# A mixture of experts that scatters its weighted rows into the output itself

## The chip, the core and the metric

The kernel runs on one core of one Trainium2 chip. The core has five engines with queues of their own: TensorE (PE, with its weight loads as PEld), VectorE (DVE), ScalarE (ACT), GpSimd (POOL) and SyncE (SP), which here only issues transfers. They meet through semaphores alone. The metric is the time of one execution on the device in microseconds (us); lower is better.

## The reference

The program is a two-layer block over x of 16 x 128 rows of 256 numbers. Layer 0 is a cross attention and a quantised feed-forward part, layer 1 a cross attention in fp8 and a mixture of experts. Only the end of layer 1 is touched:

```python
x = x + jnp.tanh(g_xattn[1]) * _L1_xattn_ref(_layernorm(x, axis=-1), ctx_2048, ...)
x = x + jnp.tanh(g_ffn[1]) * _L1_ffn_ref(_layernorm(x, axis=-1), Wr, Win, Wout)

def _L1_ffn_ref(x, Wr, Win, Wout):
    logits = xf @ Wr.T
    scores, expert = jax.lax.top_k(logits, 2)
    weights = jax.nn.softmax(scores, axis=-1)
    gate = gate.at[jnp.arange(T)[:, None], expert].add(weights)
    for e in range(8):
        h = jax.nn.silu(xf @ Win[e].T)
        y = y + gate[:, e:e + 1] * (h @ Wout[e].T)
    return y.reshape(orig_shape)
```

So each of the 2048 rows goes to two of eight experts, and the result of a row is the attention's x plus two weighted rows.

## The kernel before, in words

x stays in SBUF for the whole program (`x_rows`, 128 partitions x 16 x 256 fp32). While the second attention ends, the rows are normalised, the two experts of each are chosen, and GpSimd scatters each row twice (once for each expert) as a packet of 259 numbers into `slots` in HBM, where every expert has a shelf. A packet carries the row's number, the first expert's code and the exponential of the gap of the scores. Slots that no row took hold a row number out of all bounds, so that a later scatter skips them. SP loads the experts' weights (8.4 MB) in 16 transfers into the place of the attention's weights.

`layer1_experts` then goes through 24 tiles: 15 wide ones of two blocks of 128 slots and 9 narrow ones of one. `SIZES` is that list and `RING` = 3 the number of buffers for loaded tiles, row numbers (`to_row`) and weighted rows (`slots_y`). A tile belongs to one expert, so no row stands in it twice. For each tile n:

- SP loads the packets (L2285). From the fourth tile on it waits until tile n - 3 is turned and its weights of the sum are worked out.
- TensorE transposes (`turn`, L2300), multiplies by the first matrix (`hidden`, L2322) and by the second (`down`, L2341). The order on TensorE is hidden(n+1), turn(n+2), down(n).
- VectorE copies the turned rows (`lift`), splits the hidden values in two halves (`parts`) and works out the target row and the share of each slot (`aim`, L2372 to L2386).
- ScalarE applies silu and writes the weighted rows to y (L2429).
- GpSimd scatters y (L2439), one indirect transfer for each block of 128 rows, into `picked` in HBM. `picked` has two halves of 2048 rows: a row's first expert writes into the first half, its second expert into the second. Hence no two scatters ever touch the same place, and none waits for another.

When all scatters have landed, SP and ACT read the two halves back in seven runs each (L2454), VectorE adds them to `x_rows` (L2475), and SP stores each run (L2461). The order on each engine is that in which the code is written. `v_x` is the semaphore that counts the finished pieces of `x_rows` in the second attention, J = 4 for each of 16 batch rows.

Of the kernel before, what the change touches and what calls it, by code (L numbers as in the profile page):

```python
# [14 lines left out]
F32 = mybir.dt.float32  # L15
# [4 lines left out]
U32 = mybir.dt.uint32  # L20
I32 = mybir.dt.int32

P = 128
B = 16
D = 256
# [187 lines left out]
def common_tiles(nc):  # L213

    t = {}
    t["x"] = nc.alloc_sbuf_tensor("x_rows", [P, B, D], F32)
    t["gates"] = nc.alloc_sbuf_tensor("gates", [P, 4], F32)
    t["ident"] = nc.alloc_sbuf_tensor("ident", [P, P], F32)
    t["ident_b"] = nc.alloc_sbuf_tensor("ident_b", [P, P], BF16)
    t["half"] = nc.alloc_sbuf_tensor("minus_half", [P, 16], F32)  # L220
    t["one_eps"] = nc.alloc_sbuf_tensor("one_eps", [P, 1], F32)
    t["eps_eps"] = nc.alloc_sbuf_tensor("eps_eps", [P, 1], F32)
    t["eps"] = nc.alloc_sbuf_tensor("eps", [P, 16], F32)
    t["token"] = nc.alloc_sbuf_tensor("token", [P, B], F32)
    t["blank"] = nc.alloc_sbuf_tensor("blank_slot", [P, SLOT], F32)
    t["slots"] = nc.dram_tensor("slots", [SLOTS, SLOT], F32, kind="Internal").ap()
    t["halves"] = nc.dram_tensor("halves", [2, P, 2, HALVES, HALF], F16, kind="Internal").ap()
    t["picked"] = nc.dram_tensor("picked", [2 * B * P, D], F32, kind="Internal").ap()
    number = nc.alloc_sbuf_tensor("token_number", [P, B], I32)
    t["wb"] = nc.alloc_sbuf_tensor("w_proj_in", [P, 2, UNITS, UNIT], F16)  # L230
    t["count"] = number
    t["most"] = nc.alloc_sbuf_tensor("most", [P, 2, B], F32)
    t["before"] = nc.alloc_sbuf_tensor("picks_before", [P, NE], BF16)
    t["shelf"] = nc.alloc_sbuf_tensor("shelf", [P, NE], F32)
    t["all_b"] = nc.alloc_sbuf_tensor("ones_b", [P, P], BF16)
    t["ident_h"] = nc.alloc_sbuf_tensor("ident_h", [P, P], F16)
    t["owner"] = nc.alloc_sbuf_tensor("tile_owner", [P, WORDS * WORD], F32)
    t["word"] = nc.alloc_sbuf_tensor("owner_word", [1, WORDS], I32)
    t["shelf_row"] = nc.alloc_sbuf_tensor("shelf_row", [1, WORDS * WORD], I32)
    return t  # L240
# [981 lines left out]
J = 4  # L1222
# [91 lines left out]
def layer1_attention(nc, a, t, ctx, bank, places, final, small):  # L1314
# [15 lines left out]
    x, gates, ident = t["x"], t["gates"], t["ident"]  # L1330
# [7 lines left out]
    rows, rowsT = over("bo0", "rows_n", [P, D]), over("q_part", "rowsT_n", [P, KD, P])  # L1338
# [7 lines left out]
    s = Pieces(nc)  # L1346
# [15 lines left out]
    pe_A, a_st, g_r = sigs("pe_A", "tensor", 4), sigs("a_st", "scalar", 3), [sig(f"g_r_{k}of3", "gpsimd", 2) for k in range(3)]  # L1362
    v_n, pe_hT, a_hT = sigs("v_n", "vector", 3), sigs("pe_headsT", "tensor", 3), sigs("a_headsT", "scalar", 3)
# [486 lines left out]
    def aside(owner):  # L1850
        return [("WP", n) for n in range(WP_EIGHTHS)] if (("WP", owner)) in s.pieces else []

    flags = {"pe_A": pe_A, "a_v": a_v, "a_hT": a_hT, "pe_out": pe_out, "r_c": r_c, "v_PT": v_PT, "v_go": v_go, "d_xs": d_xs}
    layer = Layer(s, lambda owner: part(owner, 1, 2), after,
                  lambda owner, b: rounds(ORDER1[owner], b, False), lambda owner: (2, B - AHEAD))
    return layer, starting, aside, rest_halves, flags, A, S, packet
# [381 lines left out]
TS = 2  # L2238
# [2 lines left out]
WORDS = -(-TILES // WORD)  # L2241


def layer1_experts(nc, block, a, t, out, ctx):
    def sb(name, shape, dt=F32):
        return ctx.enter_context(nc.sbuf_tensor(name, shape, dt))

    def sem(name):
        return nc.alloc_semaphore(name)

    x, gates, ident, token = t["x"], t["gates"], t["ident"], t["token"]
    slots, picked = t["slots"], t["picked"]
    win = t["win"].rearrange("p (h e k n) -> p h e k n", h=2, e=NE, k=KD)
    wout = t["wout"].rearrange("p (h e k n) -> p h e k n", h=2, e=NE, k=KF)
    ident_h = t["ident_h"]
# [7 lines left out]
    xT = sb("slotsT", [P, 2, 2 * KD * TS * P], F16)  # L2263
    h32, hh = sb("h32", [P, 2, KF * TS * P]), sb("hidden", [P, 2, 2, KF * TS * P], F16)
    y = sb("slots_y", [P, RING, TS, D])
    other, to = sb("other", [P, RING, TS]), sb("to_row", [P, RING, TS], U32)
    got, put = [sem(f"t_got{n}") for n in range(RING)], [sem(f"t_put{n}") for n in range(RING)]
    gate, part, both = sb("gate_part", [P, 1]), sb("part_of", [P, RING, TS]), sb("both_parts", [P, 2, TS])
    s_gate, s_part, c_part = sem("t_gate"), sem("t_part"), Chain(nc, "c_part", 3)
    s_turn, s_xT, s_to = sem("t_turn"), sem("t_xT"), sem("t_to")  # L2270
    s_H, s_h, s_hh, s_Y, s_y = sem("t_H"), sem("t_h"), sem("t_hh"), sem("t_Y"), sem("t_y")

    def puts(n):
        return 16 * sum(SIZES[n % RING:n:RING])

    @block.sync
    def _(e):
        e.wait_ge(t["tabled"], 1)
        e.wait_ge(t["sent"], 16 * 2 * B)
        for n, size in enumerate(SIZES):  # L2280
            if n >= RING:
                e.wait_ge(s_turn, n - RING + 1)
                e.wait_ge(s_part, n - RING + 1)
            row = e.value_load(shelf_row[0:1, n:n + 1], min_val=0, max_val=SLOTS - size * P)  # L2284
            e.dma_start(taken[:, n % RING, 0:size, :],  # L2285
                        slots[bass.ds(row, size * P), :].rearrange("(s p) w -> p s w", p=P)).then_inc(got[n % RING], 16)
# [70 lines left out]
    def _(e):  # L2357
# [7 lines left out]
        def aim(n):  # L2365
            e.wait_ge(s_gate, 1)
            e.wait_ge(s_part, n)
            size = SIZES[n]
            note = taken[:, n % RING, 0:size, :]
            if n >= RING:  # L2370
                e.wait_ge(put[n % RING], puts(n))
            e.tensor_scalar(other[:, n % RING, 0:size], note[:, :, D + 1:D + 2].rearrange("p s o -> p (s o)"),  # L2372
                            owner[:, n:n + 1], float(B * P), ALU.not_equal, ALU.mult).then_inc(s_to, 1)
            e.wait_ge(s_to, 2 * n + 1)
            e.tensor_tensor(to[:, n % RING, 0:size], note[:, :, D:D + 1].rearrange("p s o -> p (s o)"),
                            other[:, n % RING, 0:size], ALU.add).then_inc(s_to, 1)

            second = note[:, :, D + 2:D + 3].rearrange("p s o -> p (s o)")
            if n >= RING:
                e.wait_ge(s_y, n - RING + 1)  # L2380
            c_part.start(e, n)
            c_part.link(e.tensor_scalar(both[:, 0, 0:size], second, 1.0, None, ALU.add))
            c_part.link(e.reciprocal(both[:, 0, 0:size], both[:, 0, 0:size]))
            c_part.link(e.scalar_tensor_tensor(both[:, 1, 0:size], note[:, :, D + 1:D + 2].rearrange("p s o -> p (s o)"),
                                               owner[:, n:n + 1], second, ALU.is_equal, ALU.max))
            e.scalar_tensor_tensor(part[:, n % RING, 0:size], both[:, 1, 0:size], gate[:, 0:1], both[:, 0, 0:size],  # L2386
                                   ALU.mult, ALU.mult).then_inc(s_part, 1)
            c_part.end()
# [44 lines left out]
    @block.gpsimd  # L2433
    def _(e):
        for n, size in enumerate(SIZES):
            e.wait_ge(s_y, n + 1)
            e.wait_ge(s_to, 2 * n + 2)
            for h in range(size):
                e.indirect_dma_start(  # L2439
                    out=picked[:, :], out_offset=bass.IndirectOffsetOnAxis(ap=to[:, n % RING, h:h + 1], axis=0),  # L2440
                    in_=y[:, n % RING, h, :], in_offset=None, bounds_check=2 * B * P - 1,
                    oob_is_err=False).then_inc(put[n % RING], 16)


    RUNS = ((0, 1), (1, 3), (3, 6), (6, 10), (10, 13), (13, 15), (15, 16))
    back = t["wout"].bitcast(F32).rearrange("p (w b d) -> p w b d", w=2, b=B)
    s_back, s_sum, s_store = [sem(f"z_back{n}") for n in range(len(RUNS))], sem("z_sum"), sem("z_store")

    def read_back(e, which):
        for n in range(RING):  # L2450
            e.wait_ge(put[n], 16 * sum(SIZES[n::RING]))
        rows = picked.rearrange("(w b p) d -> w p b d", w=2, p=P)
        for n, (b0, b1) in enumerate(RUNS):
            e.dma_start(back[:, which, b0:b1, :], rows[which, :, b0:b1, :]).then_inc(s_back[n], 16)  # L2454

    @block.sync
    def _(e):
        read_back(e, 0)
        for n, (b0, b1) in enumerate(RUNS):
            e.wait_ge(s_sum, 2 * (n + 1))  # L2460
            e.dma_start(out[b0:b1].rearrange("b p d -> p b d"), x[:, b0:b1, :]).then_inc(s_store, 16)  # L2461
        e.wait_ge(s_store, 16 * len(RUNS))

    @block.scalar
    def _(e):
        read_back(e, 1)

    @block.vector
    def _(e):
        for n, (b0, b1) in enumerate(RUNS):  # L2470
            e.wait_ge(s_back[n], 32)
            for which in range(2):
                if which:
                    e.wait_ge(s_sum, 2 * n + 1)
                e.tensor_tensor(x[:, b0:b1, :], x[:, b0:b1, :], back[:, which, b0:b1, :], ALU.add).then_inc(s_sum, 1)  # L2475


def program(nc, a, out, phases):
# [23 lines left out]
        layers(block, first, second, between, closing, left, spent, cleared)  # L2502

    with ExitStack() as ctx:
        layer1_experts(nc, block, a, t, out, ctx)
    whole.close()
    kept.close()

# [67 lines left out]
```

## Time and profile before

| | us |
|---|---|
| median of 3 runs | 1259.28 (1255.86 to 1262.04) |
| profiled execution, its own time | 1258.14 |
| its span (first to last instruction) | 1256.2 |
| PE busy in the span | 1124.0 (89%) |
| DVE busy | 1039.6 (83%) |
| ACT busy | 918.5 (73%) |
| POOL busy | 748.0 (60%) |

Times of single events come from the profiled execution, counted from the first instruction. The median is 1.14 us above that execution's time, which in turn is 1.94 us above its span. A busy share is an average over the whole span: what a change at the end is worth has to be read from what ends last there.

### The profile page before, as it was taken

To read this page: it belongs to the slowest core of one execution; us is meant where nothing else is said; L and a number is where in the kernel's file an instruction comes from. 1 tells how busy PE (TensorE), PEld (TensorE's weight loads), DVE (VectorE), ACT (ScalarE), POOL (GpSimd) and SP (SyncE) were. 2 spreads that over 40 slices of the span, in tenths; PEclk is the share of its full clock that TensorE was granted. 3 is DMA by queue.
4 is the path that set the end of the run, shared out by engine and by line. 5 is a ranking of instruction groups with operands and counts; after the bars stand their busy time and mean duration, and the time that the engine had idled before them with its cause. 6 is when DMAs were issued, how large, how long until landed. Compare 5 with 4: busy or idle time off the path is not lost. (4 is left out here: it accounts for less than half of the span.)

```text
span 1256.2 us, 30380 instructions
## 1 busy us (share of the span) xinstructions
PE 1124.0 (89%) x8831; PEld 909.8 (72%) x8831; DVE 1039.6 (83%) x2469; ACT 918.5 (73%) x3601; POOL 748.0 (60%) x1132
## 2 busy tenths in 40 slices
PE   2689999978799999999999999998999999659992
PEld 2356666645688888888888888887887888559981
DVE  6689999987898888898898899888689888756664
ACT  3557777759899989989988998997888778223330
POOL 5368888867755665665566566565546787313331
PEclk8689999989999999999999999999999999879996
DMA  6555556531230330330230221122311000723326
GB/s 167 93 89 89 89 88 87 83 54 53 73 89 2 90 90 0 88 88 1 87 88 24 65 88 47 41 88 71 89 52 47 31 35 31 277 77 86 96 69 205
DMA packets 134167, 97.56 MB, mean 78 GB/s; under 512 B 54845, under 2 KB 127679, under 8 KB 134080
## 3 DMA queue, kind: packets, MB, share of 16 engines
q1 hardware_dynamic: 124528, 84.70, 27.7%
q0 software_dynamic: 3408, 8.45, 1.9%
q10 hardware_dynamic: 6144, 3.35, 0.9%
q8 instruction: 43, 0.70, 0.2%
q14 instruction: 44, 0.36, 0.1%
HBM read 55.02 MB, written 42.09 MB: 77 GB/s over the span
## 5 line engine op out<-in xcount | busy, mean ns | idle before, releaser
L1546 POOL TENSOR_TENSOR head_rstd<-head_rstd,minus_half 128x4 f32<-128x4 f32 x192 | 225.9, 1176 | 15.0
L1534 ACT ACTIVATE squares<-ps 128x128 bf16<-128x128 f32 x768 | 202.4, 285 | 42.2 <-PE ps L1497 34.8
L1497 PE MATMUL ps<-w_proj_in,xq 128*128 128x512 f16 (+1 forms) x1024 | 209.3, 327 | 5.9 <-ACT headsT L1570 5.3
L1626 POOL TENSOR_TENSOR prob<-prob,rinv 128x512 f32<-128x512 f32 x128 | 140.6, 1098 | 108.7 <-DVE rinv L1621 108.5
L1570 ACT ACTIVATE headsT<-ps,l_hln 128x256 f32<-128x256 f32 (+1 forms) x256 | 168.1, 690 | 30.3 <-PE ps L1561 30.3
L1613 ACT ACTIVATE prob<-ps,nmax 128x128 f32<-128x128 f32 x512 | 182.6, 391 | 9.7 <-DVE nmax L1604 8.3
L1534 ACT ACTIVATION_READ_ACCUMULATOR squares<-ps 128x1 f32 x768 | 165.2, 216 | 0.0
L1554 DVE TENSOR_TENSOR heads_n<-ps,head_rstd 128x512 f32<-128x512 f32 x192 | 131.3, 684 | 25.9 <-POOL head_rstd L1546 25.6
L1497 PEld LDWEIGHTS ps<-w_proj_in,xq 128*128 (+1 forms) x1024 | 99.9, 98 | 53.1 <-issue 8.5
L1597 PE MATMUL ps<-headsT 128*128 128x128 f32 x1024 | 137.0, 277 | 1.1 <-DVE probT L1642 0.4
L1544 POOL TENSOR_TENSOR head_rstd<-head_squares,l_head_eps 128x4 f32<-128x4 f32 x192 | 46.1, 240 | 151.9 <-ACT squares L1534 151.1
L1597 PEld LDWEIGHTS ps<-headsT 128*128 128x128 f32 x1024 | 128.9, 193 | 8.1 <-issue 5.5
L1653 PE MATMUL ps<-probT,v 128*128 128x256 f32 x512 | 132.4, 381 | 0.4 <-DVE x_rows L1133 0.4
L1702 PE MATMUL ps<-w_proj_out,catq 128*128 128x256 f16 x1024 | 123.7, 275 | 3.8 <-DVE catq L1690 3.8
L1561 PE MATMUL ps<-ident,heads_n 128*128 128x128 f32 x768 | 117.1, 275 | 5.9 <-DVE heads_n L1554 5.8
L1613 ACT ACTIVATION_READ_ACCUMULATOR prob<-ps,nmax 128x1 f32 x512 | 117.5, 230 | 0.0
L1604 DVE TENSOR_REDUCE nmax<-ps 128x4 f32<-128x512 f32 x128 | 88.1, 688 | 30.0 <-PE ps L1597 28.2
L1702 PEld LDWEIGHTS ps<-w_proj_out,catq 128*128 128x128 bf16 x1024 | 100.9, 99 | 15.8 <-DVE catq L1690 4.2
L1561 PEld LDWEIGHTS ps<-ident,heads_n 128*128 128x128 f32 x768 | 91.3, 142 | 23.7 <-DVE heads_n L1554 15.9
L1504 PE MATMUL ps<-w_proj_in,ctx_parts 128*128 128x256 f16 x768 | 104.8, 273 | 0.0
L852 DVE TENSOR_REDUCE nmax<-ps 128x4 f32<-128x512 f32 x128 | 83.3, 680 | 18.8 <-PE ps L844 18.5
L1653 PEld LDWEIGHTS ps<-probT,v 128*128 128x128 f32 x512 | 87.6, 191 | 7.2 <-issue 0.6
(320 smaller groups left out, 2588.1 us busy)
## 6 DMA issues: line engine op xcount, KB each, us to landing
slots<-blank_slot SPq DMA_DIRECT2D x12, 1554.0 KB, 8.5
halves<-half_made SPq DMA_DIRECT2D x32, 256.0 KB, 2.5
w_proj_in<-halves SPq DMA_DIRECT2D x16, 512.0 KB, 9.8
w_out_raw<-in_wprojT SPq DMA_DIRECT2D x8, 512.0 KB, 3.9
half_raw<-in_winT SPq DMA_DIRECT2D x16, 256.0 KB, 2.9
half_raw<-in_woutT SPq DMA_DIRECT2D x16, 256.0 KB, 3.1
taken<-slots SPq DMA_DIRECT2D x15, 259.0 KB, 3.4
q_rows<-q_parts SPq DMA_DIRECT2D x48, 64.0 KB
```

Of the source, the lines that this page charges most:

```text
L1497: last = e.matmul(out, xq[:, k, which, slot_at], weights(k, hl, c0, n), start=(k == 0 and hl == 0), stop=(k == KD - 1 and hl == 1))
L1504: last = e.matmul(out, cx[:, k, part, slot_at], weights(k, hl, c0, n), start=(k == 0 and part == hl == 0), stop=(k == KD - 1 and part == 1))
L1534: last = e.activation(squares[:, 4 * n + h, :], A[n][:, h * HD1:(h + 1) * HD1], ACT.Square, scale=HD1**-0.5, accum_out=hss[:, 4 * n + h:4 ...
L1546: e.tensor_tensor(hr[:, four], hr[:, four], t["half"][:, four], ALU.pow).then_inc(g_r[n].sem, 1)
L1554: e.tensor_tensor(hn[:, n, :, :], A[n][:, :].rearrange("p (h d) -> p h d", h=4), spread(hr[:, 4 * n:4 * n + 4], HD1), ALU.mult).then_inc(v ...
L1561: last = e.transpose(A[n][:, h * P:(h + 1) * P], hn[:, n, h, :], ident[:, :])
L1570: last = e.activation(hT[:, n, h0:h1, :].rearrange("p h t -> p (h t)"), A[n][:, h0 * P:h1 * P], ACT.Identity, bias=hln[:, c + 1:c + 2], sc ...
L1597: last = e.matmul(S[kind][:, h * P:(h + 1) * P], hT[:, kind, h, :], hT[:, 2, 2 * kind + h // 2, :], start=True, stop=True)
L1613: last = e.activation(prob[:, kind, h, :], S[kind][:, h * P:(h + 1) * P], ACT.Exp, bias=nmax[:, kind, h:h + 1], accum_out=rowsum[:, kind, ...
L1626: e.tensor_tensor(prob[:, kind, :, :], prob[:, kind, :, :], spread(rinv[:, kind, :], P), ALU.mult).then_inc(g_p[kind].sem, 1)
L1653: last = e.matmul(O[kind][:, g * 2 * P:(g + 1) * 2 * P], v[:, kind, g, :], probT[:, kind, 2 * g:2 * g + 2, :], start=True, stop=True)
L1702: last = e.matmul(A[1][:, 0:D], catq[:, 4 * kind + h, :], wp[:, hl, 4 * j + 16 * kind + h, :], start=(n == 0), stop=(n == 15))
```

## The change

`picked` is gone, and so are the read-back, the sums and the stores at the end. Instead SP stores `x_rows` to the output in three pieces: batch rows 0 to 5 and 6 to 11 after the loads of the experts' weights, rows 12 to 15 between the loads of tiles 2 and 3. The scatter of each block now adds its rows to those of the output (`compute_op=ALU.add`). As an addition reads its target and writes it later, a tile's scatters must not meet those of the tile before: the first scatter waits for the three stores, and each later tile's first one until the scatters of the tile before have landed. `aim` only converts the row number.

```diff
+    s_laid, STORES = sem("t_laid"), ((0, 6), (6, 12), (12, 16))
+    def lay(e, n):
+        b0, b1 = STORES[n]
+        e.wait_ge(v_x.sem, v_x.at(J * b1 - 1))
+        e.dma_start(out[b0:b1].rearrange("b p d -> p b d"), x[:, b0:b1, :]).then_inc(s_laid, 16)
     @block.sync
     def _(e):
+        lay(e, 0)
+        lay(e, 1)
         e.wait_ge(t["tabled"], 1)
         e.wait_ge(t["sent"], 16 * 2 * B)
         for n, size in enumerate(SIZES):
+            if n == RING:
+                lay(e, 2)
...
-            e.tensor_scalar(other[:, n % RING, 0:size], note[:, :, D + 1:D + 2].rearrange("p s o -> p (s o)"),
-                            owner[:, n:n + 1], float(B * P), ALU.not_equal, ALU.mult).then_inc(s_to, 1)
-            e.wait_ge(s_to, 2 * n + 1)
-            e.tensor_tensor(to[:, n % RING, 0:size], note[:, :, D:D + 1].rearrange("p s o -> p (s o)"),
-                            other[:, n % RING, 0:size], ALU.add).then_inc(s_to, 1)
+            e.tensor_copy(to[:, n % RING, 0:size], note[:, :, D:D + 1].rearrange("p s o -> p (s o)")).then_inc(s_to, 1)
...
             e.wait_ge(s_y, n + 1)
-            e.wait_ge(s_to, 2 * n + 2)
+            e.wait_ge(s_to, n + 1)
+            if n == 0:
+                e.wait_ge(s_laid, 16 * len(STORES))
+            else:
+                e.wait_ge(put[(n - 1) % RING], puts(n - 1) + 16 * SIZES[n - 1])
             for h in range(size):
                 e.indirect_dma_start(
-                    out=picked[:, :], out_offset=bass.IndirectOffsetOnAxis(ap=to[:, n % RING, h:h + 1], axis=0),
-                    in_=y[:, n % RING, h, :], in_offset=None, bounds_check=2 * B * P - 1,
-                    oob_is_err=False).then_inc(put[n % RING], 16)
+                    out=sums, out_offset=bass.IndirectOffsetOnAxis(ap=to[:, n % RING, h:h + 1], axis=0),
+                    in_=y[:, n % RING, h, :], in_offset=None, bounds_check=B * P - 1,
+                    oob_is_err=False, compute_op=ALU.add).then_inc(put[n % RING], 16)
-    RUNS = ((0, 1), (1, 3), (3, 6), (6, 10), (10, 13), (13, 15), (15, 16))
-    back = t["wout"].bitcast(F32).rearrange("p (w b d) -> p w b d", w=2, b=B)
-    def read_back(e, which):
...
+    @block.sync
+    def _(e):
         for n in range(RING):
             e.wait_ge(put[n], 16 * sum(SIZES[n::RING]))
...
-    @block.vector
-    def _(e):
-        for n, (b0, b1) in enumerate(RUNS):
-            e.wait_ge(s_back[n], 32)
...
-                e.tensor_tensor(x[:, b0:b1, :], x[:, b0:b1, :], back[:, which, b0:b1, :], ALU.add).then_inc(s_sum, 1)
```

What stands on SP's queue where the expert stage begins, before the change (`halves` are the experts' weights in HBM, `shelf_row` the table of where each tile begins):

```order
243 L2175 DMA w_proj_in<-halves 128x2048 x16
244 L2276 UNCONDITIONAL_BRANCH
245 L2284 TENSOR_LOAD shelf_row
246 L2284 ISA x2
247 L2285 ISA
248 L2285 DMA taken<-slots 128x2x259
```

And after it:

```order
243 L2174 DMA w_proj_in<-halves 128x2048 x16
244 L2281 UNCONDITIONAL_BRANCH
245 L2279 DMA out<-x_rows 128x6x256 x2
246 L2293 TENSOR_LOAD shelf_row
247 L2293 ISA x2
248 L2294 ISA
249 L2294 DMA taken<-slots 128x2x259
```

Two stores now stand between the weights and the first tile's load. GpSimd's end, with the semaphores that an instruction waits for (their numbers are used a second time here and they carry the name of the first use: `v_part` and `d_ins` are `s_y` and `s_to`), before:

```order
651 L2439 DMA picked<-slots_y,to_row 4096x256 [waits v_part,d_ins]
652 L2439 DMA picked<-slots_y,to_row 4096x256
653 L2439 DMA picked<-slots_y,to_row 4096x256 [waits v_part,d_ins]
654 L2439 DMA picked<-slots_y,to_row 4096x256
655 L2439 DMA picked<-slots_y,to_row 4096x256 [waits v_part,d_ins]
```

And after (`d_int` is `s_laid`; `p_rstd`, `p_xn` and `pe_xT` are the three `put`):

```order
651 L2448 DMA out<-slots_y,to_row 2048x256 [waits d_int,v_part,d_ins]
652 L2448 DMA out<-slots_y,to_row 2048x256
653 L2448 DMA out<-slots_y,to_row 2048x256 [waits p_rstd,v_part,d_ins]
654 L2448 DMA out<-slots_y,to_row 2048x256
655 L2448 DMA out<-slots_y,to_row 2048x256 [waits p_xn,v_part,d_ins]
```

The number of scatters and their order are the same; each tile's first one has a third wait.

## Rows read from the trace of the kernel before

**Rows 1.** The page, part 2: TensorE's busy tenths in 40 slices.

```profile
PE   2689999978799999999999999998999999659992
```

**Rows 2.** The chain of waits at the end: start us, us, what.

```profile
1232.59 0.48 ACT slots_y L2429
...
1233.84 2.07 DMA picked<-slots_y,to_row
...
1237.41 9.46 DMA w_proj_in<-picked
```

**Rows 3.** Stretches: us, busy time of each engine, PEclk, DMA share, GB/s.

```profile
1085.00:1090.00 5.00, 3.36 (x16) 2.22 (x16) 3.60 (x16) 0.00 (x0) 0.00 (x0) 0.66 1.03 419
...
1240.00:1245.00 5.00, 0.00 (x0) 0.00 (x0) 2.62 (x4) 0.00 (x0) 0.00 (x0) 0.50 1.03 323
```

**Rows 4.** SP at the end: its timeline, and its wait (total, times, longest).

```profile
1240.30 13.43 SPq L2461 DMA_DIRECT2D out<-x_rows  x7
...
SPq L2506 <- DMA out<-x_rows: 2.1, 1, 2.1
```

**Rows 5.** The chain of waits within a wide tile.

```profile
1177.72 0.45 PE ps_T L2300 x8
1178.17 2.62 PE ps_Y L2341 x24
1180.79 2.62 PE ps_H L2322 x24
```

**Rows 6.** GpSimd's timeline: first pair and last two scatters, idle before in brackets.

```profile
1125.59 0.97 POOL L2439 DMA_INDIRECT picked<-slots_y,to_row  x1 [19.21 <-ACT slots_y L2429]
1126.87 0.98 POOL L2439 DMA_INDIRECT picked<-slots_y,to_row  x1 [0.30 <-issue]
...
1231.61 0.97 POOL L2439 DMA_INDIRECT picked<-slots_y,to_row  x1 [2.41 <-DVE to_row L2375]
1233.84 0.97 POOL L2439 DMA_INDIRECT picked<-slots_y,to_row  x1 [1.26 <-ACT slots_y L2429]
```

**Rows 7.** VectorE's groups, 1113 to 1235: count, busy us, mean ns, idle before.

```profile
L2363 DVE COPY slotsT<-ps_T 128x1024 f16<-128x1024 f16 (+1 forms) x24 | 14.2, 592 | 36.7 <-PE ps_T L2300 36.7
...
L2372 DVE TENSOR_SCALAR other<-taken,tile_owner 128x2 f32<-128x2 f32 (+1 forms) x24 | 5.2, 217 | 0.0
...
L2375 DVE TENSOR_TENSOR to_row<-taken,other 128x2 uint32<-128x2 f32 (+1 forms) x24 | 3.8, 160 | 0.8
```

**Rows 8.** Timelines of SP and VectorE; the last weights' issue to landing.

```profile
1076.56 8.13 SPq L2175 DMA_DIRECT2D w_proj_in<-halves  x16
...
w_proj_in<-halves SPq DMA_DIRECT2D x1, 512.0 KB, 16.4
...
1089.64 0.48 DVE L1710 SCALAR_TENSOR_TENSOR x_rows<-ps,l_out_gate,x_rows 128x256 f32<-128x256 f32 x1 [0.95 <-PE ps L1702]
...
1109.17 113.19 SPq L2285 DMA_DIRECT2D taken<-slots  x24
```

**Rows 9.** Scatters into slots: issued at 1093.0 (issue to landing), and the last one.

```profile
slots<-r_packet,r_at_u POOLq DMA_INDIRECT x1, 5.9
...
1105.40 2.70 DMA slots<-r_packet,r_at_u
```

**Rows 10.** Scatters to picked, issue to landing: issued at 1132.5, 1166.7 and 1206.2.

```profile
picked<-slots_y,to_row POOLq DMA_INDIRECT x1, 3.1
picked<-slots_y,to_row POOLq DMA_INDIRECT x1, 4.5
picked<-slots_y,to_row POOLq DMA_INDIRECT x1, 4.4
```

**Rows 11.** VectorE's timeline: the row numbers of the last tile but one.

```profile
1230.90 0.16 DVE L2375 TENSOR_TENSOR to_row<-taken,other 128x1 uint32<-128x1 f32 x1
```

**Rows 12.** The queue of GpSimd's transfers; loads of narrow tiles, issue to landing.

```profile
q0 software_dynamic: 3408, 8.45, 1.9%
...
taken<-slots SPq DMA_DIRECT2D x6, 129.5 KB, 2.1
```

More of the change, by code:

```diff
@@ L227, in common_tiles @@
     t["halves"] = nc.dram_tensor("halves", [2, P, 2, HALVES, HALF], F16, kind="Internal").ap()
-    t["picked"] = nc.dram_tensor("picked", [2 * B * P, D], F32, kind="Internal").ap()
     number = nc.alloc_sbuf_tensor("token_number", [P, B], I32)
@@ L1851, in aside @@
         return [("WP", n) for n in range(WP_EIGHTHS)] if (("WP", owner)) in s.pieces else []
-    flags = {"pe_A": pe_A, "a_v": a_v, "a_hT": a_hT, "pe_out": pe_out, "r_c": r_c, "v_PT": v_PT, "v_go": v_go, "d_xs": d_xs}
+    flags = {"pe_A": pe_A, "a_v": a_v, "a_hT": a_hT, "pe_out": pe_out, "r_c": r_c, "v_PT": v_PT, "v_go": v_go, "d_xs": d_xs, "v_x": v_x}
     layer = Layer(s, lambda owner: part(owner, 1, 2), after,
@@ L2241, with layer1_experts @@
 WORDS = -(-TILES // WORD)
-def layer1_experts(nc, block, a, t, out, ctx):
+def layer1_experts(nc, block, a, t, out, v_x, ctx):
     def sb(name, shape, dt=F32):
@@ L2249, in sem @@
         return nc.alloc_semaphore(name)
-    x, gates, ident, token = t["x"], t["gates"], t["ident"], t["token"]
-    slots, picked = t["slots"], t["picked"]
+    x, gates, ident = t["x"], t["gates"], t["ident"]
+    slots, sums = t["slots"], out.rearrange("b p d -> (b p) d")
     win = t["win"].rearrange("p (h e k n) -> p h e k n", h=2, e=NE, k=KD)
@@ L2265, in layer1_experts @@
     y = sb("slots_y", [P, RING, TS, D])
-    other, to = sb("other", [P, RING, TS]), sb("to_row", [P, RING, TS], U32)
+    to = sb("to_row", [P, RING, TS], U32)
     got, put = [sem(f"t_got{n}") for n in range(RING)], [sem(f"t_put{n}") for n in range(RING)]
@@ L2436, in _ @@
             e.wait_ge(s_y, n + 1)
-            e.wait_ge(s_to, 2 * n + 2)
+            e.wait_ge(s_to, n + 1)
[3 more added lines that the diff above has]
+                e.wait_ge(put[(n - 1) % RING], puts(n - 1) + 16 * SIZES[n - 1])
             for h in range(size):
                 e.indirect_dma_start(
-                    out=picked[:, :], out_offset=bass.IndirectOffsetOnAxis(ap=to[:, n % RING, h:h + 1], axis=0),
-                    in_=y[:, n % RING, h, :], in_offset=None, bounds_check=2 * B * P - 1,
-                    oob_is_err=False).then_inc(put[n % RING], 16)
-    RUNS = ((0, 1), (1, 3), (3, 6), (6, 10), (10, 13), (13, 15), (15, 16))
-    back = t["wout"].bitcast(F32).rearrange("p (w b d) -> p w b d", w=2, b=B)
-    s_back, s_sum, s_store = [sem(f"z_back{n}") for n in range(len(RUNS))], sem("z_sum"), sem("z_store")
-    def read_back(e, which):
+                    out=sums, out_offset=bass.IndirectOffsetOnAxis(ap=to[:, n % RING, h:h + 1], axis=0),
[3 more added lines that the diff above has]
+    def _(e):
         for n in range(RING):
             e.wait_ge(put[n], 16 * sum(SIZES[n::RING]))
-        rows = picked.rearrange("(w b p) d -> w p b d", w=2, p=P)
-        for n, (b0, b1) in enumerate(RUNS):
-            e.dma_start(back[:, which, b0:b1, :], rows[which, :, b0:b1, :]).then_inc(s_back[n], 16)
-    @block.sync
-    def _(e):
[L2458 to L2466, printed above, removed]
-    @block.vector
-    def _(e):
-        for n, (b0, b1) in enumerate(RUNS):
-            e.wait_ge(s_back[n], 32)
-            for which in range(2):
-                if which:
-                    e.wait_ge(s_sum, 2 * n + 1)
-                e.tensor_tensor(x[:, b0:b1, :], x[:, b0:b1, :], back[:, which, b0:b1, :], ALU.add).then_inc(s_sum, 1)
 def program(nc, a, out, phases):
@@ L2504, in program @@
     with ExitStack() as ctx:
-        layer1_experts(nc, block, a, t, out, ctx)
+        layer1_experts(nc, block, a, t, out, flags["v_x"], ctx)
     whole.close()
```

## The prediction

> **What bounds the kernel now.** I read the page first. Its slices show a PE that is busy almost everywhere, and a gap and a tail late in the span [rows 1]; after the last `slots_y` there is no matmul at all. Then the chain of waits, which says what stands in that tail: the last weighted rows leave ScalarE at 1233.1, the last scatter lands at 1235.9, and then come the reading back of both halves of `picked` [rows 2], the sums on VectorE and the stores. The stretches by window show that this tail is a transfer: the DMA engines are fully busy at 323 GB/s while PE is at 0 [rows 3]. The last store lands at 1253.7 + 2.1 = 1255.8 [rows 4], and the span ends 0.4 later. So everything from 1235.9 to 1255.8, 19.9 us, is the tail that the change removes.
>
> Ahead of it the expert stage runs at PE's pace. A wide tile (two blocks) takes 0.45 + 2.62 + 2.62 = 5.69 us of transposes, down and hidden matmuls, with no gap [rows 5]. GpSimd's timeline shows the scatters: a pair for each of 15 wide tiles, then nine single ones, the last two only 2.2 us apart [rows 6]. Today nobody needs a scatter to be done before the ring of three comes round, so its latency is free. That is what the change ends.
>
> **What it removes.** The read-back, the 14 sums and the seven stores behind the last scatter: 19.9 us. On VectorE two small operations (217 and 160 ns) become one copy; VectorE waits 36.7 us in all for PE in this stage [rows 7], so I count 0 for them.
>
> **What it adds before the experts.** Three stores of x, 2.1 MB. The first two (1.57 MB) are issued by SP right behind the 16 weight loads, at 1084.7. The last of these loads is issued at about 1084.3 and lands 16.4 us later [rows 8], at 1100.7. At the 420 GB/s of that stretch [rows 3] the stores take 3.7 us more, to 1104.4. The rows of x they need are long final: the very last is written at 1090.1 [rows 8], and these two stores end at batch row 12. Sharing the DMA engines with them are GpSimd's last scatters into `slots`; SP waits for these before the first tile is loaded. Beside the full queue one landed in 5.9 us, the last of them in 2.7; that is issued at 1105.4, after the stores are through [rows 9], and the first tile's load follows at 1109.2 [rows 8]. Cost 0; if the stores run a few us late, the last scatter lands like its loaded sisters, up to 3 us later, and the first tile with it. The third store (512 KB) stands on SP behind the loads of tiles 0 to 2 and ahead of that of tile 3, which waits for the first tile to be turned anyway. The first scatter waits for it too, but that comes only at 1125.6 [rows 6], when such a store has had over 10 us. Cost 0.
>
> **What it adds to each tile.** The scatters now add into rows which an earlier tile may have written, so every tile's first scatter waits until the last one of the tile before has landed. The scatters become one chain from 1125.6 to the end. Behind the waiting scatter nothing else stands on GpSimd; who waits for it is ScalarE (its y buffer) and VectorE (`aim`), both three tiles later. The chain is a sum:
> - 15 pairs, second behind first by 1.28 us [rows 6]: 19.2 us.
> - The last scatter of each of 24 tiles, issue to landing. The view of DMA issues, asked for each, gives 2.1 to 4.5 us; the second ones of pairs, which share the engines with the load of a coming tile, average 3.16, the nine single ones 2.7. All 24 together: 71.7 us. Of them a usual pair's second, 3.1, and the two highest are in [rows 10]; the last, 2.07, is in [rows 2].
> - 23 times the time from a landing to the next scatter's start. The trace has no such wait. From VectorE's `to_row` (ends 1231.06) to the scatter it takes 0.55 us, from ScalarE's last (ends 1233.08) 0.76, between two scatters with no wait 0.30 [rows 6, 11, 2]. I take 0.55: 12.7 us.
>
> 1125.6 + 19.2 + 71.7 + 12.7 = 1229.2, against 1235.9 today. So with scatters as quick as now the chain would just about keep up: laid out tile by tile with each scatter's own time of readiness, it ends at 1236.9. Only a few us are to spare, and each of 24 links gets longer by what an added read of the destination costs. Call it D. The end is then about 1229.2 + 24 D once D is over 0.5 (below this the scatters still wait for PE now and then: D = 0 gives 1236.9, D = 0.34 gives 1240.3).
>
> **How large is D?** No accumulating transfer is in the trace. Not below zero, since the write is the same and a read comes on top. From below: queue 0 moved 71 indirect scatters in 1.9% of the span, 0.34 us of every DMA engine for each [rows 12]; twice the reading at most doubles this, so 0.34 if latency and issue stay. With GpSimd making half as many descriptors again, 0.98 us of its time [rows 6] grow by 0.49, twice in a pair: (15 x 0.98 + 9 x 0.49)/24 + 0.34 = 1.14. From above: the read stands wholly ahead of the write, like a load of one block from `slots`, 2.1 us [rows 12]. The middle of 0.34 and 1.14 with a little for the read's own latency is 0.8, and I take that; the ends 0 and 2.1 stay for the range.
>
> The Trainium skill ("Collectives: The Full Stack", "Why ReduceScatter is half of AllGather") says that a reducing DMA reads two sources through one ring and is slower for the second read, not for the adding; no run here shows that. By it D would be the 0.34 above. Against the change speaks "DMA: Bandwidth & Descriptors" ("Anatomy of one DMA"): about 2.0 us of a DMA are fixed, nearly all of it the receipt of the write, and are to be hidden behind other work; here a chain pays them 24 times. The trace agrees for scatters that stand alone (2.1), and shows more for pairs beside a load. The page's 2.0 + bytes/436e3, 2.3 us for 131 KB, in place of the 71.7 us measured would give a chain with ample slack.
>
> **Sum.** The last scatter lands at 1229.2 + 24 x 0.8 = 1248.4, where today the last store lands at 1255.8: the span becomes 1248.8, 7.4 us less. The profiled execution took 1258.14 (1.94 around its span), the median of the three runs is 1259.28, 1.14 above it. So 1250.7 for a profiled run, 1251.8 for the median.
>
> **Rivals.**
> 1. *The chain hides.* D up to 0.5. The scatter's own latency is mostly fixed, and 0.34 is all the engines need. In its favour also: a scatter that starts late falls less often beside the load of a coming tile, and could land in the 2.1 us of the last one. Then the last landing is at 1237 to 1241.5, the median 1240 to 1245. Against it: even today's latencies leave only 6.7 us of room.
> 2. *The chain becomes the bound and eats the tail's gain.* One mechanism: the wait of each tile's first scatter for the previous landing, 24 times D. It decides from D = 1.11, where 1229.2 + 24 D reaches 1255.8. With D = 1.5 the last landing is at 1265.2, median 1268.6; with the serial read, D = 2.1, 1279.6 and 1283. For it speak the generation on GpSimd, which a pair pays twice, and the 4.1 to 4.5 us of single scatters in the trace, which now stand on the chain. ScalarE and then PE would stall behind it.
> 3. *The early stores delay the first tile.* Up to 3 us on top of any case: 1255 in place of 1251.8. Against it, the 1.0 us between the end of the stores and the last scatter's issue.
>
> **Chances.** The forecast's case, the chain binds but leaves the time at or under today's within what can be told, D from 0.5 to 1.38 (median 1245 to 1265.7): 0.48. Rival 1: 0.20. Rival 2, D over 1.38: 0.32. Rival 3 comes on top of any, 0.1. A measurement of this kernel tells about 0.5% from no change, 6.3 us: below 1253.0 is faster, above 1265.6 slower. Below 1253.0 means D under 0.85: rival 1 and 0.26 of the forecast's case, 0.46. From there to D = 1.38 nothing would be told, the other 0.22 of the forecast's case. Beyond, rival 2: 0.32. The range holds D from 0.1 to 1.8: 1240 to 1276; the forecast's case alone 1245 to 1266.
>
> **What would show it.** `taken` loads still start at about 1109 and PE's first expert matmuls at 1113 to 1115 (else rival 3). The chain of waits ends in DMA `out<-slots_y,to_row`, with neither read-back nor sums behind it. On GpSimd the idle time ahead of the scatters goes to that DMA and no more to ScalarE; where the pairs stay 5.7 us apart, rival 1 is right, and where they spread to 6 us and more, rival 2. The issue-to-landing of the new scatters, less that of today, is D, with GpSimd's duration of one (0.97 now) as its part. The prediction is wrong if D is under 0.3 or over 1.2, or if the tail behind the last `slots_y` is longer than 6 us for another reason than the chain.

## The result: slower by 1%, and the profile after

| | before | after |
|---|---|---|
| median, us | 1256.7 (6 runs, 1255.39 to 1262.04) | 1270.14 (6 runs, 1266.56 to 1273.37) |
| ratio after to before | | 1.0098, 95% interval 1.0082 to 1.0113 |
| span of the profiled execution | 1256.2 | 1271.6 |
| first scatter of the expert stage starts | 1125.6 | 1128.0 |
| last scatter starts | 1233.8 | 1264.0 |
| stage, first to last scatter's start | 108.2 | 135.9 |
| end of GpSimd's last instruction to the end of the span | 21.4 | 6.1 |

The forecast was 1251.8 and faster, in a range of 1240 to 1276. The time lies in the range, but on the other side of no change: the interval of the ratio lies wholly above 1. (The median of before is of six runs, the three quoted above among them. The execution profiled after is the slowest of its six, 1273.37.)

The tail is gone, as [rows 2, 3] let expect: no read-back, no sums. The stage has grown by 27.7 us. GpSimd's timeline at its start and its end, to be held against [rows 6] (start, duration, in brackets the idle time before):

```profile
1128.02 1.58 POOL L2448 DMA_INDIRECT out<-slots_y,to_row  x1 [18.62 <-ACT slots_y L2434]
1129.90 1.71 POOL L2448 DMA_INDIRECT out<-slots_y,to_row  x1 [0.30 <-issue]
1134.64 1.60 POOL L2448 DMA_INDIRECT out<-slots_y,to_row  x1 [3.02 <-DMA out<-slots_y,to_row]
...
1203.90 1.54 POOL L2448 DMA_INDIRECT out<-slots_y,to_row  x1 [3.03 <-DVE to_row L2381]
1205.74 1.55 POOL L2448 DMA_INDIRECT out<-slots_y,to_row  x1 [0.31 <-issue]
1210.35 1.54 POOL L2448 DMA_INDIRECT out<-slots_y,to_row  x1 [3.05 <-DVE to_row L2381]
...
1259.36 1.55 POOL L2448 DMA_INDIRECT out<-slots_y,to_row  x1 [2.05 <-DMA out<-slots_y,to_row]
1263.95 1.54 POOL L2448 DMA_INDIRECT out<-slots_y,to_row  x1 [3.04 <-DMA out<-slots_y,to_row]
```

An adding scatter keeps GpSimd for 1.54 us and more (39 of them average 1.57) where a plain one took 0.97, so the second of a pair starts 1.86 us behind the first instead of 1.28. From one pair to the next it is 1210.35 - 1203.90 = 6.45 us, where PE needs 5.69 [rows 5].

The chain of waits shows one such link:

```profile
1203.90 1.54 POOL out L2448
1205.44 0.31 issue
1205.74 3.74 DMA out<-slots_y,to_row
...
1209.63 0.49 issue
...
1210.35 1.54 POOL out L2448
```

The pair's second scatter starts on GpSimd at 1205.74, lands 3.74 us later at 1209.48 (a landing is counted from that start, so it includes GpSimd's own 1.55 us), and the next tile's first one starts 0.87 us behind that. So between tiles everything waits for this one sequence of issue, landing and issue. Note the releaser that the timeline names in the middle of the stage, `DVE to_row`: an inference that would mislead. That `to_row` is the one for the tile two further on; VectorE's `aim` was waiting for the same landing, followed it by 0.1 us, and so was the last event before the scatter. The distance from landing to scatter is 0.81 to 0.91 us in 22 of 23 links, whichever engine is named.

The stretches show PE giving way: full at first, then busy for 26.39 of 34 us where it was 31.00 in the same stretch before (us, busy PE, PEld, DVE, ACT, POOL, granted clock, DMA share, GB/s):

```profile
1130.00:1160.00 30.00, 30.00 (x297) 27.12 (x295) 19.13 (x54) 10.17 (x20) 14.43 (x9) 1.00 0.51 87
1200.00:1234.00 34.00, 26.39 (x254) 20.37 (x251) 14.34 (x50) 7.75 (x15) 15.59 (x11) 0.95 0.37 59
```

The queue of GpSimd's transfers over the whole span, which answers to [rows 12] (packets, MB, share of 16 engines' time):

```profile
q0 software_dynamic: 7152, 8.45, 3.5%
```

The bytes are the same, the packets are not. [Rows 12] mixes the scatters into `slots` with those of the expert stage, so here are the 39 of the stage alone, before in 1120 to 1237, after in 1120 to 1269:

```profile
q0 software_dynamic: 1872, 4.20, 9.9%
```

```profile
q0 software_dynamic: 5616, 4.20, 22.3%
```

Divided by 39, a plain scatter is 48 packets and an adding one 144. In time it is 9.9% of 117 us against 22.3% of 149 us: 0.30 us of every DMA engine for a plain scatter and 0.85 for an adding one.

At the very end SP waits, after the last landing, for the closing of the program (engine, line, waited for: us in total, times, longest):

```profile
SPq L2456 <- DMA out<-slots_y,to_row: 21.8, 1, 21.8
...
SPq L2487 <- PEq L2487: 4.2, 1, 4.2
```

Before, that last wait was 0.2 us. The early stores cost nothing that shows: from the last piece of `x_rows` to the first tile's load it is 1112.08 - 1092.67 = 19.4 us, and was 1109.17 - 1089.64 = 19.5 [rows 8].

```profile
1092.67 0.48 DVE L1709 SCALAR_TENSOR_TENSOR x_rows<-ps,l_out_gate,x_rows 128x256 f32<-128x256 f32 x1 [1.19 <-PE ps L1701]
...
1112.08 2.71 SPq L2294 DMA_DIRECT2D taken<-slots  x3
```

One reading ahead of the result was wrong here, at no price: the rows that the two stores need were called long final, but the view of SP's waits has it wait 3.4 us for VectorE's `x_rows` ahead of them. The 3.0 us by which both events come later than before arose ahead of anything that the change touches: SP's loads of the experts' weights already start at 1079.36, against 1076.56 [rows 8]. Over the ten profiled executions of this study the first scatter starts anywhere between 1121.4 and 1128.8, so I compare the stage's length and not its position.

### The profile page after: what moved, and what is told of

Same layout as the page of the kernel before. It is cut to its first block and busy times, and to the rows that moved or that the text cites. A ratio compares the mean times of both kernels' runs of the same rounds, so it can differ in the third digit from the quotient of the medians.

```text
span 1271.6 us, 30323 instructions
## 1 busy us (share of the span) xinstructions
PE 1133.2 (89%) x8831; PEld 911.1 (72%) x8831; DVE 1023.6 (80%) x2431; ACT 916.6 (72%) x3601; POOL 768.3 (60%) x1132
## 5 line engine op out<-in xcount | busy, mean ns | idle before, releaser
L2448 POOL DMA_INDIRECT out<-slots_y,to_row x39 | 61.3, 1571 | 94.8 <-DVE to_row L2381 56.6
```

## The experiments

Theory A after the result: the chain of 24 links is the bound, and what makes it too long is the addition (on GpSimd, on the DMA engines and in the landing). All ratios are to the kernel before, run beside each kernel.

**1. The addition left out, the chain kept.**

```diff
-                    oob_is_err=False, compute_op=ALU.add).then_inc(put[n % RING], 16)
+                    oob_is_err=False).then_inc(put[n % RING], 16)
```

> The changed kernel with the addition left out of the scatters (each scatter overwrites its rows, so the output lacks x and one of the two weighted rows); the waits of the chain and the early stores stay. Theory A, the price is the addition, paid on every link: scatter back to 0.97 us on GpSimd, second of a pair 1.28 behind the first, landings back to about 3.2 and 2.7, link from landing to start 0.87 as measured after the change. The chain then ends at 1239.7 + the 2.4 us by which the changed kernel's stage began later = 1242, median about 1246 to 1249, some 22 us under the changed kernel. Rival B, the price is the waiting itself, whatever the transfer does: no less than 1262.

Measured: 1244.98, a microsecond below the expected range, ratio 0.9893 (0.9876 to 0.9909); the stage takes 111.5 us. Rival B falls. GpSimd's timeline (columns as above):

```profile
1166.78 0.97 POOL L2448 DMA_INDIRECT out<-slots_y,to_row  x1 [3.45 <-ACT slots_y L2434]
1168.06 0.97 POOL L2448 DMA_INDIRECT out<-slots_y,to_row  x1 [0.30 <-issue]
1172.68 0.97 POOL L2448 DMA_INDIRECT out<-slots_y,to_row  x1 [3.65 <-DMA out<-slots_y,to_row]
```

Here the tile at 1166.8 was held up by ScalarE, the one at 1172.7 by a landing and comes 0.2 us late: plain scatters in a chain all but keep up with PE (111.5 us of stage against 108.2 before), as the sum ahead of the result said.

**2 and 3. No chain: adding scatters, and plain ones, to rows of their own.** Both aim at the 4096 rows of the old `picked`; `x_rows` is stored early and nothing is read back. VectorE's two operations for the row number are those of the kernel before. The plain run also leaves out `compute_op=ALU.add`.

```diff
-            if n == 0:
-                e.wait_ge(s_laid, 16 * len(STORES))
-            else:
-                e.wait_ge(put[(n - 1) % RING], puts(n - 1) + 16 * SIZES[n - 1])
...
-                    out=sums, ...
+                    out=t["picked"][:, :], ...
```

> The changed kernel with the adding scatters aimed at the 4096 distinct rows of the old buffer picked, so that no scatter meets another, and with no waits between tiles; the output is then x alone. Theory A: GpSimd's pair takes 3.7 of the 5.69 us, PE sets the pace again, stage ends 1 us later than plain scatters: median 1243 to 1247. Rival C, the adding transfers themselves are too slow for the stage even unchained (by the DMA engines or GpSimd): over 1255.

> As the one before, with plain scatters too: the kernel before with its tail (read-back, sums) left out and the stores early; the output is x alone. It says what the removal of the tail is worth by itself: by the trace 19.9 us, less whatever stands between the last landing and the end. If the 4.4 us seen there after the change belong to GpSimd's last scatter, the median is 1256.7 - 19.9 + 4 = 1241; if they belong to the addition or the chain, 1237.

Measured: adding 1242.46, half a microsecond below the expected range, ratio 0.9875 (0.9859 to 0.9892), stage 107.8; plain 1242.52, ratio 0.9885 (0.9869 to 0.9902), stage 108.5. Rival C falls: without the chain the addition costs nothing that can be told, though each of its scatters still holds GpSimd longer. GpSimd's group of scatters in the adding run and then the plain one (count, busy us, mean ns, idle before and its releasers):

```profile
L2449 POOL DMA_INDIRECT picked<-slots_y,to_row x39 | 60.6, 1553 | 67.8 <-ACT slots_y L2439 49.0 <-DVE to_row L2385 12.8 <-issue 5.4
```

```profile
L2449 POOL DMA_INDIRECT picked<-slots_y,to_row x39 | 38.1, 978 | 90.2 <-ACT slots_y L2439 69.2 <-DVE to_row L2385 16.2 <-issue 4.9
```

In both the releasers are the engines that make the data. The plain run also prices the removal of the tail alone: 1257.7 - 1242.5 = 15.2 us (14.5 by the ratio), not 19.9. SP's last wait in it:

```profile
SPq L2488 <- PEq L2488: 4.7, 1, 4.7
```

**4. Adding scatters to rows of their own, chained at a distance of one.** As 2, with the wait for the tile before put back (that for the early stores stays out), so that no addition meets another one's rows but the order is the changed kernel's.

```diff
+            if n:
+                e.wait_ge(put[(n - 1) % RING], puts(n - 1) + 16 * SIZES[n - 1])
```

> The adding scatters aimed at distinct rows of picked as in e2, but with each tile waiting for the landing of the one before, as in the changed kernel; the output is x alone. Theory A: the chain alone makes the time, so 1267 to 1272, like the changed kernel. Rival D, additions into rows that another tile has written shortly before are what is slow: then well under the changed kernel, below 1260.

Measured: 1271.29, ratio 1.0110 (1.0093 to 1.0126), stage 137.6. That is the changed kernel's time. Rival D falls: for the time it does not matter which rows are added to. Experiments 1 to 4 side by side: plain and unchained 1242.5, adding and unchained 1242.5, plain and chained 1245.0, adding and chained 1271.3. The chain by itself costs 2.5 us and the addition by itself nothing; only the two together cost 28.8.

**5. The chain at a distance of two.**

```diff
+            if n >= 2:
+                e.wait_ge(put[(n - 2) % RING], puts(n - 2) + 16 * SIZES[n - 2])
```

> The adding scatters aimed at distinct rows, each tile waiting for the landing of the tile two before it; the output is x alone. Theory A, a chain of links of 6.7 us (wide) and 4.4 us (narrow): with a distance of two the scatters may be 2 x 5.69 us apart from their condition and are never held up, so the time is that of no waits at all, 1240 to 1245. Rival E, any wait for a landing slows GpSimd's issue (a fixed price of about 0.9 us a tile even when it is met): 1250 and more.

Measured: 1244.01, ratio 0.9898 (0.9880 to 0.9916), stage 108.8 us. One wait fewer (22 in place of 23), each one tile further back, and the price is gone. Rival E falls.

**6 and 7. What stands behind the last landing.** The kernel before with one more scatter by GpSimd at the very end, and, as control, with one more store by SP.

```diff
+    @block.gpsimd
+    def _(e):
+        e.wait_ge(s_store, 16 * len(RUNS))
+        e.indirect_dma_start(
+            out=picked[:, :], out_offset=bass.IndirectOffsetOnAxis(ap=to[:, (TILES - 1) % RING, 0:1], axis=0),
+            in_=y[:, (TILES - 1) % RING, 0, :], in_offset=None, ...).then_inc(s_late, 16)
...
```

```diff
+        e.dma_start(picked[0:P, :], y[:, (TILES - 1) % RING, 0, :]).then_inc(s_late, 16)
+        e.wait_ge(s_late, 16)
```

> The kernel before with one more plain scatter of 128 rows (the last tile's, again) issued by GpSimd after the last store has landed, and waited for. Its own cost is link 0.9 + landing 2.2 = 3.1. If the 4.4 to 4.7 us from the last landing to the end belong to an execution that ends with GpSimd's work (theory F), they come on top, less the 0.4 there are now: 1257.7 + 3.1 + 4.2 = 1265. If they belong to the chain's or the addition's aftermath (rival G): 1261.

> The kernel before with one more plain store of 128 rows issued by SP after all others, and waited for: the control of the run with the late scatter. Both theories: some 2.5 us more than before, 1260, with 0.4 us behind the landing.

Measured: the scatter 1266.44, ratio 1.0062 (1.0039 to 1.0085), 8.6 us between the medians (by the ratio 7.8); the store 1259.10, ratio 1.0017 (1.0003 to 1.0030). SP's waits at the end of the run with the scatter, then of that with the store:

```profile
SPq L2520 <- PEq L2520: 4.8, 1, 4.8
SPq L2520 <- DMA picked<-slots_y,to_row: 2.8, 1, 2.8
```

```profile
SPq L2513 <- DMA picked<-slots_y: 1.4, 1, 1.4
SPq L2513 <- PEq L2513: 0.2, 1, 0.2
```

Theory F holds, and more sharply than it was put. In all eight profiles whose last work is a scatter by GpSimd, plain or adding, chained or not, the span ends 6.1 to 6.2 us after GpSimd's instruction ends. In the run with the late scatter:

```profile
1259.97 0.97 POOL L2473 DMA_INDIRECT picked<-slots_y,to_row  x1 [21.59 <-DMA out<-x_rows]
```

1259.97 + 0.97 + 6.2 = 1267.1, its span. In the changed kernel it is 1263.95 + 1.54 + 6.1 = 1271.6. SP's last wait, which begins when it has seen the last landing, varies from 4.2 to 4.8 us over the eight, so the end keeps its distance from GpSimd's instruction and not from the landing. That a shorter landing would not have ended these executions sooner follows from this, but no run tried it. What the engines do in these 6.1 us no view shows, and it stays open.

**8. A version that beats both.** Two tiles of one expert share no row. So a tile need wait for the tile before only where that one belongs to another expert, and otherwise for the one two before it (experiment 5: free). The first four tiles keep the changed kernel's waits. VectorE writes a table of 24 numbers, and from the fifth tile on GpSimd reads from it whether the expert changes and waits for a semaphore value worked out from that.

```diff
+        e.tensor_tensor(differ[0:1, 1:TILES], owner[0:1, 1:TILES], owner[0:1, 0:TILES - 1], ALU.not_equal).then_inc(s_differ, 1)
...
+            if n >= 4:
+                other_expert = e.value_load(differ[0:1, n:n + 1], min_val=0, max_val=1)
...
+                e.wait_ge(put[(n - 2) % RING], puts(n - 2) + 16 * SIZES[n - 2])
+                e.wait_ge(put[(n - 1) % RING], other_expert * (16 * SIZES[n - 1]) + puts(n - 1))
+                e.tensor_tensor(idle[:, n:n + 1], t["eps"][:, 0:1], t["half"][:, 0:1], ALU.add)
```

(The small operation on GpSimd only carries the wait.)

> The changed kernel, complete, with the wait for the tile before only where that tile belongs to another expert (two tiles of one expert share no row); otherwise a tile waits for the one two before it. GpSimd reads from a small table whether the expert changes, for each tile from the fifth on. With these inputs 8 of the 14 links between wide tiles fall within an expert (experts fill 5, 4, 3, 10, 3, 4, 4 and 4 blocks). Theory A: at each change the chain falls 1.0 us behind PE and within an expert it catches up, so the wide tiles keep PE's pace, the last narrow ones cost 5 us of lag; last landing about 1242, 4.5 us to the end, median 1247 to 1252, under the kernel before. Rival H: reading the table and the register waits cost a microsecond or more on GpSimd at each tile, or the landings get longer when two tiles' additions overlap: 1256 or more.

Measured, with the complete output: 1247.88, ratio 0.9933 (0.9914 to 0.9951); stage 113.0 us. Its timeline within one expert's tiles and across a change:

```profile
1159.48 0.77 POOL L2457 TENSOR_TENSOR idle<-eps,minus_half 128x1 f32<-128x1 f32 x1
1160.41 1.56 POOL L2459 DMA_INDIRECT out<-slots_y,to_row  x1 [0.16 <-issue]
1162.27 1.55 POOL L2459 DMA_INDIRECT out<-slots_y,to_row  x1 [0.30 <-issue]
1163.28 0.77 POOL L2457 TENSOR_TENSOR idle<-eps,minus_half 128x1 f32<-128x1 f32 x1
1164.20 1.58 POOL L2459 DMA_INDIRECT out<-slots_y,to_row  x1 [0.16 <-issue]
...
1178.40 0.19 POOL L2457 TENSOR_TENSOR idle<-eps,minus_half 128x1 f32<-128x1 f32 x1 [2.31 <-DMA out<-slots_y,to_row]
1179.10 1.60 POOL L2459 DMA_INDIRECT out<-slots_y,to_row  x1 [0.52 <-issue]
```

Within an expert the pairs follow at 3.8 us and take back what the changes lose; at a change the landing is waited for. Rival H falls. How much it gains should depend on how the rows fall on the experts; only these inputs were run.

## Why the prediction was wrong, step by step

The picture was right: a tail of transfers that the change removes, and 24 tiles' scatters in a chain with almost nothing to spare. What came is what rival 2 describes, the chain eating the tail's gain, but not on its terms: a slowdown that can be told was put at D over 1.38, and D, what an addition makes each link longer, is 1.18. That is past the 1.11 from which the gain was to be gone, yet inside the forecast's case, and under the 1.2 that was named as a sign of being wrong. So the steps that failed are three terms of the sum, all too small: D, the link, and the closing time. The sum missed by 22.8 us of span (1248.8 against 1271.6), in three terms and one shift:

- **D, the price of an addition in each link: 9.0 us.** Forecast 0.8, measured (28.0 - 19.2 for the pairs' gaps + 91.1 - 71.7 for the landings of each tile's last scatter)/24 = 1.18. The upper of the two estimates, 1.14, was near, with its parts wrongly shared out. An addition costs GpSimd 0.59 us more a scatter, not 0.49, and as a landing includes GpSimd's time this makes 39 x 0.59/24 = 0.96 of the 1.18, where the estimate had 0.80; what is left for reading, engines and landing is 0.22 in place of 0.34. (The DMA engines are busy 0.55 us longer with each scatter, but over half of this does not show in the landing.) I took the middle of two numbers with no reason against the higher, at a place where 24 times the difference turns the sign.
- **The link from a landing to the next scatter: 7.4 us.** 23 links of 0.87 make 20.1; forecast 23 x 0.55 = 12.7. I had three rows, 0.30, 0.55 and 0.76, and took the middle one, measured from a VectorE instruction; the true one lies above all three. No row of before had a wait for a landing on GpSimd.
- **The end: 4.0 us.** Forecast 0.4 us behind the last landing, measured 4.4. With SP's store last it had been 0.4; with GpSimd's scatter last it is 6.1 behind that instruction. Removing the tail was worth 15.2 us (experiment 3) where I counted 19.9. The sum moved the end to another engine and kept the old closing time.
- **The shift: 2.4 us**, the stage's later beginning in this one execution, is no effect of the change.

9.0 + 7.4 + 4.0 + 2.4 = 22.8.

How much each failure weighs: with the measured D and all else as forecast the span is 1229.2 + 28.3 + 0.4 = 1257.9, 1.7 above that of before; with the forecast D and the measured link and closing it is 1248.8 + 7.4 + 4.0 = 1260.2. So either would have turned the sign alone, D by little. With the true link and closing the chain decides from D = (1256.2 - 1241.0)/24 = 0.63 on (1241.0 = 1125.6 + 19.2 + 71.7 + 20.1 + 4.4), not from 1.11. That the time lies in the range all the same is luck: the range was made from D alone, and the 11.4 us of the other two terms were not in it.

What held: the shorter `aim` counted at nothing (experiment 4 keeps the two operations and takes the changed kernel's time); the early stores at nothing (rival 3 falls, 19.4 us against 19.5); the chain with plain scatters, 111.5 us of stage measured where the tile-by-tile layout with today's landings and the true link of 0.87 gives 112. Rival 1 did not come: the second of a wide pair lands in 3.96 us on average (3.16 before), the single ones in 3.52 (2.70), and a later start brought no relief from the loads.

On the pages of the Trainium skill: "Collectives: The Full Stack" ("Why ReduceScatter is half of AllGather") has the reducing transfer pay for its second read alone. Here the DMA engines' time per scatter grows 2.9 times (0.85 against 0.30 us), in three times the packets, so the trace shows more than a doubling. The Trainium skill's "DMA: Bandwidth & Descriptors" ("Rules for kernel authors") wants a DMA issued early and waited for late, so that its fixed cost lies beside other work. The runs agree: experiment 5 puts each landing beside the next tile's work, and the 1271.29 us of experiment 4 become 1244.01.

## What to carry to other kernels

When a change turns independent transfers into a chain, add up a whole link: issue time, landing, and wake-up, and set it against the pace of the stage; where the slack of a link is under the uncertainty of its largest term, the sign is open however large the removed work is. The cure is distance: one more step between a transfer and whoever waits for it made the same additions free (experiment 5, on rows of their own), and what may be apart is a question of the data (here tiles of one expert). Price a removed tail by what then ends last, the closing of that engine included.

## What the runs showed of the hardware

- An indirect scatter of 128 rows of 1 KB that adds: 1.57 us on GpSimd on average against 0.98, 144 packets against 48, 0.85 us of each DMA engine against 0.30, and 0.8 us more from its start on GpSimd to the landing, of which GpSimd's own time is 0.59.
- From the landing of a scatter to the next one that waits for it on GpSimd: 0.87 us on average, 0.81 to 0.91 in 22 links of 23.
- The span ended 6.1 to 6.2 us after the end of GpSimd's last scatter instruction, in eight profiles of eight whose last work that was. With SP's store last (the kernel before) it ended 0.4 us behind the landing.
